# An attention and mixture-of-experts kernel: totals behind the routing, low weights in two parts, unread products in TensorE's waits, and the states' masks ahead of the scans

## The reference

```python
q = exp(x @ Wq.T + bq); k = exp(x @ Wk.T + bk); v = x @ Wv.T + bv       # per head
kv = cumsum(k[..., :, None] * v[..., None, :], axis=1)
k1 = cumsum(k, axis=1)
out = einsum('zsD,zsDd->zsd', q, kv) / sum(q * k1, axis=-1)
x = layernorm(x + out @ Wo.T + bo)
scores = sigmoid(x @ gate_w.T); choice = scores + gate_bias
# 2 of 4 groups of experts by the sum of their two best, then the 8 best experts in them
w = 2.5 * scores[top8] / (sum(scores[top8]) + 1e-20)
final = sum(w * (silu(x @ wg.T) * (x @ wu.T)) @ wd.T over the top 8) + shared(x)
x = layernorm(x + final)
```

## Time and profile before

| | |
|---|---|
| median of 3 runs | 462.87 us (462.61 to 464.24) |
| the profiled execution | 463.29 us, of which 461.5 us are the span of its instructions |
| TensorE busy | 424.0 us (92% of the span) |
| VectorE busy | 347.4 us (75%) |
| ScalarE busy | 273.3 us (59%) |
| GpSimd busy | 282.4 us (61%) |
| longest wait of GpSimd for a transfer | 10.7 us, at 52.02 |

### The profile page before, as it was taken

The page is one execution under the profiler, slowest core; times in us unless marked ns, Lnnn a source line. Parts: engine busy times, 40 slices in busy tenths (PEclk is TensorE's granted clock), DMA queues, the critical chain, the costliest instruction groups (busy, mean ns, idle before and its releaser), DMA issues.

```text
span 461.5 us, 10791 instructions
## 1 busy us (share of the span) xinstructions
PE 424.0 (92%) x3954; PEld 324.8 (70%) x3954; DVE 347.4 (75%) x909; ACT 273.3 (59%) x530; POOL 282.4 (61%) x208
## 2 busy tenths in 40 slices
PE   5855799999999999999999999999999999899982
PEld 3733587778867787778877787778877787578761
DVE  2678548797878968797878968796878968777652
ACT  3835334963587546963587546963587546555642
POOL 2565236864676557864677557764677557757781
PEclk9989589999999999999999999999999999999996
DMA  7400544346440823446340923446440913466500
GB/s 233 187 1 1 147 92 90 92 97 141 93 113 7 197 69 82 91 103 135 91 116 12 202 68 74 90 104 134 91 116 9 200 41 81 91 134 129 121 11 23
DMA packets 28660, 45.08 MB, mean 98 GB/s; under 512 B 1984, under 2 KB 10304, under 8 KB 28224
## 3 DMA queue, kind: packets, MB, share of 16 engines
q1 hardware_dynamic: 28608, 44.40, 41.2%
HBM read 41.77 MB, written 2.62 MB: 96 GB/s over the span
## 4 chain that ended last, share of the span: by engine, by line
PE 40%; DVE 32%; issue 12%; POOL 8%; ACT 2%; DVEq 1%; ACTq 0%; POOLq 0%
PE bank L326 39%; DVE units L866 7%; POOL units L958 5%; DVE stats L741 2%; DVE hidden_lo L721 2%; POOL rstd L977 2%; DVE top_of_group L782 2%; DVE x L753 2%; DVE bank L775 1%; ACT hidden_hi L584 1%; DVE replaced L814 1%; DVE out_sb L878 1%; DVE k_sum L847 1%; DVE probs L731 1%; DVE kv_blocks L836 1%
## 5 line engine op out<-in xcount | busy, mean ns | idle before, releaser
L958 POOL TENSOR_TENSOR units<-units,weight_wide 128x512 f32<-128x512 f32 x128 | 174.3, 1367 | 130.5 <-DVE units L866 115.9
L602 ACT ACTIVATE units<-bank 128x512 f32<-128x512 f32 x136 | 80.7, 594 | 79.2 <-PE bank L326 78.9
L866 DVE TENSOR_TENSOR units<-bank,units 128x512 f32<-128x512 f32 x136 | 92.9, 683 | 35.1 <-PE bank L326 28.0
L584 ACT ACTIVATE hidden_hi<-units 128x512 fp32r<-128x512 f32 x136 | 86.1, 634 | 53.7 <-POOL units L958 47.7
L721 DVE TENSOR_TENSOR hidden_lo<-units,hidden_hi 128x512 fp32r<-128x512 f32 x112 | 97.7, 873 | 19.6 <-ACT hidden_hi L584 18.8
L326 PE MATMUL bank<-x_hi,gate_hi 128*128 128x512 f32 x136 | 62.1, 457 | 2.0 <-DVE units L866 1.6
L326 PE MATMUL bank<-hidden_hi,down_hi 128*128 128x512 f32 x136 | 55.0, 404 | 1.7 <-DVE hidden_lo L721 1.7
L326 PE MATMUL bank<-x_hi,up_hi 128*128 128x512 f32 x136 | 54.7, 403 | 1.8 <-ACT units L602 1.8
L326 PE MATMUL bank<-x_lo,gate_hi 128*128 128x512 f32 x136 | 54.6, 401 | 0.0
L326 PE MATMUL bank<-x_hi,gate_lo 128*128 128x512 f32 x136 | 54.4, 400 | 0.0
L326 PE MATMUL bank<-x_hi,up_lo 128*128 128x512 f32 x136 | 54.1, 398 | 0.0
(11 more groups left out here) (107 smaller groups left out, 670.8 us busy)
## 6 DMA issues: line engine op xcount, KB each, us to landing
weight_wide<-weight_d SPq DMA_DIRECT2D x62, 512.0 KB, 6.7
xT<-xT_in SPq DMA_DIRECT2D x8, 256.0 KB, 6.8
x_tok<-x_in SPq DMA_DIRECT2D x8, 256.0 KB, 6.9
out_dram<-out_sb SPq DMA_DIRECT2D x8, 256.0 KB, 2.3
weight_wide<-up_in SPq DMA_DIRECT2D x1, 1088.0 KB, 9.0
up_raw<-up_in SPq DMA_DIRECT2D x1, 1088.0 KB, 11.0
down_raw<-down_in SPq DMA_DIRECT2D x1, 1088.0 KB, 13.2
weight_d<-weightT SPq DMA_DIRECT2D x8, 64.0 KB, 1.6
```

Source lines behind the costliest of these rows:

```text
L584: nc.scalar.activation(hidden_hi[place(n, g)][:, :], units[place(n, g)][:, :], ACT.Copy).then_inc(hidden_hi_done, 1)
L602: nc.scalar.activation(units[place(n, g)][:, :], up_banks[2 * n % 3][:, :], ACT.Silu).then_inc(silu_done, 1)
L866: V.tensor_tensor(units[place(n, g)][:, :], up_banks[(2 * n + 1) % 3][:, :], units[place(n, g)][:, :], ALU.mult).then_inc(gated_done, 1)
L958: G.tensor_tensor(units[place(n, g)][:, :], units[place(n, g)][:, :], weight_wide[:, (n - 1) % (2 * PIECE), :], ALU.mult).then_inc(hidden_ ...
```

## The change

Five things. The scans of group 1 move on VectorE from in front of the routing to behind the second units, and with them GpSimd's product of q and totals, which now stands behind the first units weighted by the load. The low parts of gate and up are made in two pieces each, nine blocks early and eight late, and `up(9)` waits for the late ones. TensorE makes products of `wqT` with `attn_w` that nothing reads (`keep_warm`, 19 in all, into the bank `y_bank`), at seven places in the prologue. From group 2 on the states are masked in slot 14, ahead of the scans, and no longer in slot 15. In the last group that is routed (m = 7) the exponentials are turned one slot later; and block 0's high and low part in group 0 are made one slot later.

```diff
+EARLY_BLOCKS = 9
+EARLY_COLS, LATE_COLS = slice(0, 128 * EARLY_BLOCKS), slice(128 * EARLY_BLOCKS, 128 * BLOCKS)
+WARM = {"x1": 6, "x1T": 2, "up": 1, "weight": 4, "den": 3, "between": 2}
...
-            if g == 0 and n in (2, 3):
-                return (1, 2) if n == 3 else ()
+            if g == 0 and n in (1, 2, 3):
+                return ((), (0,), (1, 2))[n - 1]
...
+            def keep_warm(count):
+
+                for _ in range(count):
+                    mm(y_bank[:, 0:256], wqT, attn_w[:, 0:256])
+
...
+                if ffn and g == 0 and n in (1, 2):
+                    keep_warm(WARM["up"])
                 if ffn:
                     up(n, g, u)
...
                 if mid and n == 10:
+                    if m == 0:
+                        keep_warm(WARM["x1T"])
                     pe.wait_ge(x1T_copied, reached(m + 1))
...
-                if mid and not front and n == 10:
+                if mid and not front and n == (10 if m == 0 else 11):
                     turn_exponentials(m)
...
                     pe.wait_ge(qk_sum_done, reached(m + 1))
+                    if m == 1:
+                        keep_warm(WARM["den"])
...
                 if mid and n == 2:
+                    if m == 1:
+                        keep_warm(WARM["between"])
                     between_chunks(m, 0)
...
                 if mid and n == 9:
+                    if m == 0:
+                        keep_warm(WARM["x1"])
                     pe.wait_ge(x1_done, reached(m + 1))
...
                 if mid and n == 14:
+                    if m == 0:
+                        keep_warm(WARM["weight"])
                     pe.wait_ge(weight_done, reached(m + 1))
...
+                if front and f > 1 and n == 14:
+                    masked_states(f)
                 if front and f != 1 and n == 14:
                     k_totals(f)
...
-                if m == 0 and mid and n == 8:
+                if m == 0 and mid and n == 14:
                     k_totals(1)
-                if front and f != 1 and n == 15:
+                if front and f == 0 and n == 15:
                     masked_states(f)
...
-                if mid and m == 0 and n == 10:
+                if mid and m == 0 and n == 14:
                     q_times_totals(1)
...
-                    pool.wait_ge(gate_split, 1)
-                    G.tensor_tensor(gate_lo[:, :], gate_raw, gate_hi[:, :].bitcast(F32), ALU.subtract
-                                    ).then_inc(gate_split, 1)
-                if g == -1 and mid and n == 7:
...
+                    weight_lows(gate_lo, gate_raw, gate_hi, gate_split, EARLY_COLS)
+                    weight_lows(up_lo, up_raw, up_hi, up_split, EARLY_COLS)
+                    weight_lows(gate_lo, gate_raw, gate_hi, gate_split, LATE_COLS)
+                if g == -1 and mid and n == 9:
+                    weight_lows(up_lo, up_raw, up_hi, up_split, LATE_COLS)
```

More of the change, by code:

```diff
@@ L294, in load_first @@
                 sp.sem_inc(apart, 1)
-                sp.wait_ge(gate_split, 2)
+                sp.wait_ge(gate_split, 3)
                 sp.sem_inc(apart, 1)
@@ L336, in up @@
                     pe.wait_ge(x1_lo_done, reached(g + 1))
-                if g == 0 and n == 0:
-                    pe.wait_ge(gate_split, 2)
-                    pe.wait_ge(up_split, 2)
+                if g == 0 and n in (0, EARLY_BLOCKS):
+                    pe.wait_ge(gate_split, 2 if n == 0 else 3)
+                    pe.wait_ge(up_split, 2 if n == 0 else 3)
                 cols = slice(128 * n, 128 * n + 128)
@@ L941, in rows_and_bias, with weight_lows @@
                                 ).then_inc(x_bias_done, 1)
+            def weight_lows(low, raw, high, split, cols):
+                pool.wait_ge(split, 1)
+                G.tensor_tensor(low[:, cols], raw[:, cols], high[:, cols].bitcast(F32), ALU.subtract
+                                ).then_inc(split, 1)
             def q_times_totals(f):
@@ L995, in slot @@
                     rows_and_bias(0)
-                    pool.wait_ge(gate_split, 1)
-                    G.tensor_tensor(gate_lo[:, :], gate_raw, gate_hi[:, :].bitcast(F32), ALU.subtract
-                                    ).then_inc(gate_split, 1)
-                if g == -1 and mid and n == 7:
-                    pool.wait_ge(up_split, 1)
-                    G.tensor_tensor(up_lo[:, :], up_raw, up_hi[:, :].bitcast(F32), ALU.subtract
-                                    ).then_inc(up_split, 1)
+                    weight_lows(gate_lo, gate_raw, gate_hi, gate_split, EARLY_COLS)
[3 more added lines that the diff above has]
+                    weight_lows(up_lo, up_raw, up_hi, up_split, LATE_COLS)
                 if g == -1 and mid and n == 10:
```

## The result

Before 463.21 us (median of 4 runs), the changed kernel 472.85 us (4 runs, 472.62 to 475.35): ratio 1.022, 95% interval 1.020 to 1.0245. The forecast was 458.5, with a range to 462.3. The profiled execution took 473.04 us, its span is 471.3 (before 461.5).

What follows compares the result with a forecast made beforehand. TensorE was taken as the bound, busy 51.11 of a middle group's 51.6 us. Prologue -1.9, masks -2.9 and last turn +0.4 sum to -4.4; against the 462.87 median this gave 458.5 us, range 456.3 to 462.3.

Steps and rivals of the forecast that it cites:

- The unread products ... all inside waits: Prologue: the 19 extra TensorE products fit inside existing waits, 0.2 us late at most; their worth is keeping the clock full.
- (d): Prologue: the load does not advance with the routing; up(3) done at 68.0, sum +3.5, 466.4 us; 5%.
- Masks, -2.9 forecast: Groups 2 to 7: masking states ahead of the scans removes TensorE's whole wait at the group's end, 6 x 0.48 us.
- low part 14 to 151.6: End of a middle group: VectorE's second low part ends at 151.6, so units 16 finish at 152.2 us.
- rival (c): Masks' gap does not close, as low part 14 needs a queued high part; sum -3 to -1.5, 459.9 to 461.4; 10%.
- Prologue, -1.9 forecast: Start of the run: earlier routing and load let up(3) end at 60.1 instead of 62.0; bounds -2.4 to -1.5 us.
- Write and load keep their distance: Prologue: from weights copied to GpSimd's first multiplication stays 5.36 us, so that multiplication starts at 47.9, 4.1 us earlier.
- my bounds of 3.4 and 5.8: Prologue: the full clock returns 3.4 us after work sets in or 5.8 after the last wait, at 54.0 to 56.4.
- rival (b): Prologue: the clock comes back late because scores are small products; sum -2.5 to -0.6, 460.4 to 462.3 us; 22%.
- on which the prologue hangs: GpSimd's product of q and totals, placed behind the first loaded multiplication, ends at 50.6; TensorE stands 4.7 us, losing its clock.
- The turn: +0.4 forecast: Last routed group: turning the exponentials later ends at 394.2 instead of 393.83, delaying VectorE's routing; costs 0.4 us.

Runs made afterwards that it cites:

- +196: 196 TensorE instructions more than before's: changed kernel plus 30 tiny products, 465.27 us; with product ahead of load, masks back and 34 tiny products, 458.39 us.

## Why the prediction was wrong

**No term for the code.** The step that failed is "The unread products ... all inside waits", which cost them as TensorE's time alone. Their time was indeed hidden, but each is also four instructions that TensorE must be fed. Two groups grew by 9.1 us: 5.2 in the stands (2.65 and 2.57), 1.7 twice for the 3.4 us at half clock behind each, 0.13 twice for the masks; 0.2 I can't account for. None of the four rivals was this one; (d), slower, had 5% and another mechanism. The trace of before had the hint: a queue of 31 code packets that shares 16 engines with loads of 512 KB, and a packet that started 2.87 us before TensorE reached the place where it would stand. I did not look at that queue. Without the stands the change is still no gain (465.27 us with +196, 0.4% above before), for the two steps that follow.

**Masks, -2.9 forecast, nothing measured.** The step "low part 14 to 151.6" failed. In the changed kernel, the end of the middle group:

```profile
150.05 1.27 POOL L986 TENSOR_TENSOR units<-units,weight_wide 128x512 f32<-128x512 f32 x1 [1.55 <-DVE units L886]
150.24 1.63 DVE L741 TENSOR_TENSOR hidden_lo<-units,hidden_hi 128x512 fp32r<-128x512 f32 x1 [0.27 <-ACT hidden_hi L604]
151.79 0.68 DVE L886 TENSOR_TENSOR units<-bank,units 128x512 f32<-128x512 f32 x1
152.62 0.47 PE L329 MATMUL bank<-x_hi,gate_hi 128*128 128x512 f32 x1 [0.43 <-DVE units L886]
```

The low part could start earlier, and did, but it ended at 151.87, 0.55 us after GpSimd's multiplication (151.32), and 0.6 is what it takes alone. This group started 0.41 us earlier than in before, so the forecast's 151.6 would be 151.2 here, and the low part is 0.7 late. Before's trace had the same ends: its two low parts there ended at 149.43 and 151.93, each 0.54 or 0.55 behind a multiplication (148.88 and 151.39). I had used the rule of the Trainium skill (SBUF — State Buffer, Who interferes with whom) on the scans and found it true there; the same rule for an operation with two SBUF inputs, applied to this one, gives the measured end. That was my rival (c), 10%, by another reason: a wait that changed its name. It even costs 0.13 us a group (51.73 for 51.60).

**Prologue, -1.9 forecast, -0.4 measured** (105.13 against 105.54 for the first second scores; +1.7 in the change itself with +196). The first steps held: routing from 32.24 (32.4 forecast), weights done at 41.10 (41.3), scans of 1.26 us together, copy at 42.06 (42.0). The load did not keep its distance: GpSimd started at 49.52, not 47.9, and its product ended at 52.0, not 50.6.

```profile
49.52 1.26 POOL L986 TENSOR_TENSOR units<-units,weight_wide 128x512 f32<-128x512 f32 x1 [9.63 <-DMA weight_wide<-weight_d]
50.74 1.26 POOL L975 TENSOR_TENSOR k_sum<-k_sum,qT 128x512 f32<-128x512 f32 x1
```

The first multiplication waits for the first two of six loads alone. It started 4.99 us after the first of them was issued, in place of 3.48. SyncE's timeline after, and under it that of before:

```profile
42.74 0.34 SPq L278 DMA_DIRECT2D weight_d<-weightT  x1
44.53 4.71 SPq L303 DMA_DIRECT2D weight_wide<-weight_d  x6
```

```profile
46.76 0.34 SPq L275 DMA_DIRECT2D weight_d<-weightT  x1
48.54 3.75 SPq L300 DMA_DIRECT2D weight_wide<-weight_d  x6
```

The second load took 4.35 us from issue to landing (45.10 to 49.45) in place of 2.84, and that is 1.5 of the 1.6 us. A packet of TensorE's code started at 47.22, while this load was under way; in before none started between 33 and 56 us. In the seven kernels in which a packet started 1.7 to 2.1 us behind the issue of this load, it took 4.0 to 4.4 us; in the five without one, 2.8 to 3.1 (in the other two the packet started 0.2 and 0.4 us behind the issue: 4.0 and 3.2). Two experiments turn it on and off. The kernel before started its first multiplication 3.48 us after the first issue, and 5.04 us with 76 instructions added; the changed kernel 4.99 us, and without unread products 3.58 us (issued at 44.87):

```profile
48.45 1.26 POOL L986 TENSOR_TENSOR units<-units,weight_wide 128x512 f32<-128x512 f32 x1 [8.28 <-DMA weight_wide<-weight_d]
```

So here, too, the unread products cost time by their code. The step that failed is "Write and load keep their distance". The longer issue (4.71 us in place of 3.75) is one instruction, the fifth, which took 1.59 us in place of some 0.6, also beside that packet, but nothing waited for it here. TensorE then:

```profile
52.05 2.92 PE L329 MATMUL bank<-attn_w 128*128 128x256 f32 x6 [6.24 <-POOL k_sum L975]
54.91 0.66 PE L329 MATMUL bank<-k_sum,const 128*32 128x128 f32 x8
56.05 1.20 PE L329 MATMUL bank<-q_heads,kT 32*64 32x128 f32 x64 [0.49 <-ACT den_cols L699]
...
59.99 0.50 PE L329 MATMUL bank<-x_hi,gate_hi 128*128 128x512 f32 x1
```

Windows of that stretch (the clock is the third column from the end):

```profile
50.00:56.00 6.00, 3.51 (x14) 2.05 (x14) 0.00 (x0) 0.28 (x1) 3.22 (x3) 0.50 0.99 211
56.00:62.00 6.00, 5.95 (x148) 5.19 (x149) 3.65 (x6) 0.98 (x2) 0.00 (x0) 0.99 0.62 126
```

The clock fell to 1.2 GHz in this wait and was back just behind 56, some 4 us after work set in, between my bounds of 3.4 and 5.8; the products take 1.20 us for the scores (2.02 before). In this trace the clock was as forecast. In others of the same prologue it came back later (half from 47.9 for 13.7 us with the smaller load, from 47.5 to 61.2 with 30 tiny products in this wait), and their first second scores start at 107.8 and 107.2. That is rival (b): it is seen in two of the traces with this prologue, and what decides it is not shown. Moving the product ahead of the load, with unread products kept (+196), brings 100.11: 5.0 us better than the changed kernel, by the term that I had called the one "on which the prologue hangs".

**The turn: +0.4 forecast, +0.38 measured.**

## What to carry to other kernels

Before instructions are added to an engine that is never idle, count them against the packets of its code, and look when those packets land beside the large loads; an unread product that costs no time can still cost microseconds two hundred later. If a stand has no releaser, count records up to it: a fixed remainder says code. And where one operation was seen to end only behind another (VectorE's low part behind GpSimd's multiplication), ask when the other one ends, not when this one can start.

## What the runs showed of the hardware that I had not expected

- A code packet of 16 KB (256 instructions of TensorE) was held up while loads of 512 KB took all DMA engines (the groups at 214 and 271 us; with a quarter of the bytes it was not). TensorE ran dry 193 records past a multiple of 256, in each of eleven stands of over 1.3 us in eight kernels (records 449, 1217, 1473, 3265, 4289, 5313, 7361), and went on 2.35 to 2.61 us after the start of its packet (3.05 in one).
- The disturbance goes the other way too. Of the 1358 transfers that SyncE issued behind 40 us in the fourteen traces, 64 took over 1.0 us to issue (the common size is 0.5 to 0.6), and beside every one of them a packet of TensorE's code had started, from 0.74 us before the issue began to 0.21 behind that.
- The length of a stand did not decide whether the clock fell. Stands of 2.57, 2.65 and 2.39 us, and one of 2.16 in the kernel without unread products, were followed by 3.4 us at half clock (the two groups of the changed kernel: 4.5 us longer); stands of 2.02, 2.03, 2.09 and, in before with 76 instructions, 2.86 us were not (2.3 to 3.2 us longer). That is also why, in these traces, those 76 instructions alone cost less than the whole change.
- In the wait for the weights the clock fell at 41.45 while 28 tiny products of 32x1 ran (40.32 to 42.71); with eight records of 128x256 in the same wait (39.70 to 41.59) it stayed full.
